# Layer-1 projections with the covariance chain of one batch placed between the products of the next, and the first load for the attention moved into that stage

## What is computed

```
qkv = layernorm(x) @ W_qkv.T + b_qkv          # q, k, v: 16 heads of 8
scores = einsum('bhid,bhjd->bhij', q, k) * D ** -0.5
topk_scores, indices = top_k(scores, int(1024 * 0.3))
masked = full(-inf); masked[indices] = topk_scores
x = x + (softmax(masked) @ v) @ W_out.T + b_out
```

## Time and profile before

| | us |
|---|---|
| median of 3 runs | 3386.67 |
| lowest, highest | 3386.05, 3387.24 |
| the profiled execution, whole time | 3384.95 |
| its span in the trace | 3383.2 |
| layer-1 projections in it | 856 to 1000 |
| layer-1 attention in it | 1000 to about 3040 |

### The profile page before, as it was taken

How to read it: one execution, slowest core, us unless ns; L and a number is a source line. 1 busy time by engine, 2 the same in 40 slices (tenths; PEclk the granted TensorE clock), 3 DMA queues, 4 the chain that set the end, 5 groups by cost and what they waited for, 6 DMA issues and landing times. The chain is left out here.

```text
span 3383.2 us, 74549 instructions
## 1 busy us (share of the span) xinstructions
PE 2601.1 (77%) x23705; PEld 1456.7 (43%) x23705; DVE 2700.5 (80%) x8588; ACT 2383.1 (70%) x3987; POOL 2029.4 (60%) x4543
## 2 busy tenths in 40 slices
PE   3699999669654777777777777775777777758999
PEld 2233333234431444444444444443554454543444
DVE  5788888235438999999999999998999999744444
ACT  2266666533117999999999999997999999822221
POOL 3133333410117999999999999996999989640000
PEclk8699999879665777777778777877777777868999
DMA  5312211000121011001101100110110110010000
GB/s 150 94 47 53 55 49 40 14 25 26 52 63 21 2 18 18 11 9 18 18 2 18 18 12 9 18 18 2 18 18 2 18 18 2 2 33 3 7 7 10
DMA packets 115264, 85.87 MB, mean 25 GB/s; under 512 B 58153, under 2 KB 97339, under 8 KB 114875
## 3 DMA queue, kind: packets, MB, share of 16 engines
q1 hardware_dynamic: 106331, 75.20, 10.4%
q0 software_dynamic: 8192, 4.79, 0.9%
q10 hardware_dynamic: 352, 1.18, 0.1%
HBM read 54.25 MB, written 19.40 MB: 22 GB/s over the span
## 5 line engine op out<-in xcount | busy, mean ns | idle before, releaser
L1285 POOL TENSOR_TENSOR a_near<-a_side,a_z 128x1024 int32<-128x1024 int32 x512 | 968.9, 1892 | 42.6
L1181 PE MATMUL a_ST<-a_qs,a_ks 75*128 75x128 bf16 x4096 | 656.5, 249 | 397.5 <-DVE a_mask L1418 208.6
L1381 DVE MAX8 a_cand<-a_near 128x8 f32<-128x256 f32 x2048 | 810.8, 414 | 0.0
L1181 PEld LDWEIGHTS a_ST<-a_qs,a_ks 75*128 75x128 bf16 x4096 | 459.1, 114 | 564.1 <-DVE a_mask L1418 338.7
L1425 DVE TENSOR_SCALAR_CACHE_REDUCE a_z<-a_S,a_thr 128x1024 f32<-128x1024 f32 x512 | 650.2, 1270 | 33.6 <-POOL a_thr L1261 27.9
L1205 ACT ACTIVATE a_signs<-a_z,a_tiny 128x1024 bf16<-128x1024 f32 x512 | 589.6, 1152 | 73.9 <-DVE a_z L1425 72.4
L1198 ACT ACTIVATE a_signs<-a_S,search 128x1024 bf16<-128x1024 f32 x512 | 572.2, 1118 | 24.3 <-PE a_S L1136 24.2
L1220 ACT ACTIVATE a_eT<-a_ST 128x1024 f32<-128x1024 f32 x512 | 520.2, 1016 | 18.0 <-PE a_ST L1182 17.5
L776 ACT ACTIVATE a_eT<-a_ST 128x512 f32<-128x512 f32 (+3 forms) x768 | 329.2, 489 | 210.0 <-PE a_ST L761 148.6
L1136 PE MATMUL a_S<-a_ks,a_qs 72*128 72x512 bf16 x1024 | 394.4, 475 | 101.4 <-DVE a_z L1425 76.6
L880 DVE TENSOR_REDUCE a_mx<-a_S 128x1 f32<-128x512 f32 (+3 forms) x768 | 381.2, 547 | 77.3 <-PE a_S L748 67.7
(11 more groups left out here) (341 smaller groups left out, 4639.6 us busy)
## 6 DMA issues: line engine op xcount, KB each, us to landing
a_qs<-q_parts SPq DMA_DIRECT2D x174, 64.0 KB
a_ks<-k_parts SPq DMA_DIRECT2D x174, 64.0 KB
a_qs<-a_flip SPq DMA_DIRECT2D x512, 0.8 KB
q_parts<-p_qp SPq DMA_DIRECT2D x48, 128.0 KB, 1.7
k_parts<-p_kp SPq DMA_DIRECT2D x48, 128.0 KB, 1.8
a_qs<-q_parts SPq DMA_DIRECT2D x60, 96.0 KB
a_ks<-k_parts SPq DMA_DIRECT2D x60, 96.0 KB
f_w<-L_ffn_W SPq DMA_DIRECT2D x16, 256.0 KB, 2.8
```

The source lines that it names most:

```text
L1181: pe.matmul(ST[:, block_of], ks[:, base(hl) + kb * P:base(hl) + (kb + 1) * P], qs[:, tile(hl):tile(hl) + P], start=True, stop=False)
L1285: pool.tensor_tensor(near[:, hl % NEARS, :].bitcast(I32), side[:, one].bitcast(I32).broadcast_to([P, SEQ]), z[:, hl % H, :].bitcast(I32), ...
L1381: mm = dve.max(found[:, 8 * g:8 * g + 8], near[:, h2 % NEARS, g * SW:(g + 1) * SW])
```

## The change

`project` is split. `project0` is what it was for layer 0, with the same instructions. `project1` replaces it for layer 1, written out over chunks n = 0 to 7 and over five rounds b = 0 to 4. In round b PE and DVE do the two chunks of batch b, and the covariance chain of batch b - 1 stands in pieces between them; round 0 has no chain, round 4 has only one. To allow that there are four `qf`, two `qcq` and two `mean_bd`; `q_ps` goes from two to one, and the sums, the chain, the applied covariance and the estimates each have a PSUM bank. PE signals the queries and the keys separately (`q_done`, `k_done`). SP stores q ahead of v.

`qs`, `ks` and `v` of the attention are now allocated ahead of `project1`, and SP issues the loads of quad 0 in it, behind the stores of chunk 3, after waiting for the stores of batch 0. In `attention1` the two load calls at the start are gone.

```diff
-            project(nc, k, 1, stats, ln1)
             ctx_all = part.enter_context(nc.sbuf_tensor("ctx1", [P, NT, D], F32))
+            k.qs, k.ks = (part.enter_context(nc.sbuf_tensor(f"a1_{x}", [STACK + SPLIT, 2 * 4 * SEQ], BF16)) for x in ("qs", "ks"))
+            k.v = part.enter_context(nc.sbuf_tensor("a1_v", [P, 2, IB, 4 * (HD + 1)], F32))
+            k.kq_in, k.v_in = (part.enter_context(nc.semaphore(f"a1_{x}_in")) for x in ("kq", "v"))
+            project1(nc, k, stats, ln1)
...
+            normalize(0)
+            for b in range(B + 1):
+                n = CB * b
+                if b > 0:
+                    take_sums(b - 1)
+                if b < B:
+                    normalize(n + 1)
+                if b > 0:
+                    take_means(b - 1)
+                if b < B:
+                    split_q(n)
+                if b > 0:
+                    take_gram(b - 1)
+                if b < B:
+                    add_bias_v(n)
+                if b > 0:
+                    take_cov(b - 1)
+                if b < B - 1:
+                    normalize(n + 2)
+                if b > 0:
+                    weigh(n - 2)
+                if b < B:
+                    split_q(n + 1)
+                if b > 0:
+                    weigh(n - 1)
+                    take_estimates(n - 2)
+                if b < B:
+                    add_bias_v(n + 1)
+                if b > 0:
+                    take_estimates(n - 1)
...
+            def sum_products(n):
+                b, c = n // CB, n % CB
+                if c == 0 and b > 0:
+                    pe.wait_ge(cov_v, COV_V * (b - 1) + 2)
+                for t in range(CT):
+                    mm = pe.matmul(gram_ps, xn[c][:, t, 0:D], xn[c][:, t, :],
+                                   start=(c == 0 and t == 0), stop=(c == CB - 1 and t == CT - 1))
+                mm.then_inc(gram_s, 1)
...
+            for b in range(B + 1):
+                n = CB * b
+                if b < B:
+                    turn(n)
+                    sum_products(n)
+                if b > 0:
+                    weigh_sums(b - 1)
+                if b < B:
+                    queries(n)
+                    keys(n)
+                if b > 0:
+                    weigh_again(b - 1)
+                if b < B:
+                    values(n)
+                if b > 0:
+                    outer(b - 1)
+                if b < B:
+                    turn(n + 1)
+                    sum_products(n + 1)
+                if b > 0:
+                    apply_cov(n - 2)
+                if b < B:
+                    queries(n + 1)
+                    keys(n + 1)
+                if b > 0:
+                    estimate(n - 2)
+                    apply_cov(n - 1)
+                if b < B:
+                    values(n + 1)
+                if b > 0:
+                    estimate(n - 1)
...
+            for n in range(NCH):
+                b, c = n // CB, n % CB
+                cols = slice(c * CW, (c + 1) * CW)
+                sp.wait_ge(qsplit, SPLIT * n + SPLIT)
+                for s in range(SPLIT):
+                    sp.dma_start(k.q_parts[s, b * D:(b + 1) * D, cols], qp[c][:, s, :]).then_inc(stored[c], 16)
...
+                if n == 2 * CB - 1:
+                    for x in range(CB):
+                        sp.wait_ge(stored[x], STORES)
+                    load_quad(sp, k, 0)
+                    load_v(sp, k, 0)
...
-            load(0)
-            load_v(0)
             sp.wait_ge(const, 1)
```

More of the change, by code:

```diff
@@ L391, in _ @@
-            if lead:
-                dve.wait_ge(sd_s, 1)
-                dve.scalar_tensor_tensor(first[:, :], base1[:, :], -Z_KEEP, first[:, :], ALU.mult, ALU.add).then_inc(fin_v, 1)
-                dve.tensor_scalar(step[:, :], base1[:, :], -1.0 / (2 * SEQ * PDF_KEEP), None, ALU.mult).then_inc(fin_v, 1)
-                dve.wait_ge(fin_v, 2)
-                dve.scalar_tensor_tensor(base1[:, :], step[:, :], -SGN_KEEP, first[:, :], ALU.mult, ALU.add).then_inc(fin_v, 1)
-                dve.wait_ge(fin_v, 3)
@@ L406, in _ @@
             act.nop().then_inc(xT_s, 1)
-            if pre is None:
-                act.wait_ge(var_s, NCH)
             act.activation(std[:, :], var[:, :], ACT.Sqrt).then_inc(std_s, 1)
-            scale = QSCALE1 if lead else 1.0
             def project_chunks(b):
@@ L427, in project_chunks @@
-                    act.wait_ge(ksplit, SPLITS * n + SPLITS)
-                    act.activation(kf[c][:, :], k_ps[c % VB][:, :], ACT.Identity, bias=k.bk[layer][:, 0:1])
-                    act.activation(kp[c][:, 0, :], k_ps[c % VB][:, :], ACT.Identity, bias=k.bk[layer][:, 0:1]).then_inc(k_s, 1)
-            if layer == 0:
-                project_chunks(0)
-                project_chunks(1)
-                for c in range(CB):
-                    act.wait_ge(stored[c], free(1))
-                act.wait_ge(blank_s[0], 64)
-                load_pass0(act, k, 0)
-                project_chunks(2)
-                project_chunks(3)
-            else:
-                with act.Fori(0, B) as b:
-                    project_chunks(b)
@@ L446, in _ @@
+                    act.activation(kp[c][:, 0, :], k_ps[c][:, :], ACT.Identity, bias=k.bk[0][:, 0:1]).then_inc(k_s, 1)
+            project_chunks(0)
+            project_chunks(1)
+            for c in range(CB):
+                act.wait_ge(stored[c], free(1))
+            act.wait_ge(blank_s[0], 64)
+            load_pass0(act, k, 0)
+            project_chunks(2)
+            project_chunks(3)
         @block.gpsimd
         def _(pool):
-            for c in range(SPLITS * CB):
+            for c in range(SPLIT * CB):
@@ L452, in _ @@
                     n = b * CB + c
-                    done = SPLITS * CB + SPLITS * n
+                    done = SPLIT * CB + SPLIT * n
                     pool.wait_ge(k_s, CB + n + 1)
@@ L465, in _ @@
                 pe.nop().then_inc(v_done, 1)
-            if lead:
-                for c in range(CB):
-                    pe.nop().then_inc(gram_s, 1)
-                pe.nop().then_inc(est_s, 1)
             with pe.Fori(0, B) as b:
@@ L478, in _ @@
                     mm.then_inc(turned, 1)
-                    if lead:
-                        if c == 0:
-                            pe.wait_ge(est_v, 2 * CB * b + 1)
-                        for t in range(CT):
-                            mm = pe.matmul(gram_ps, xn[c][:, t, 0:D], xn[c][:, t, :],
-                                           start=(c == 0 and t == 0), stop=(c == CB - 1 and t == CT - 1))
-                        mm.then_inc(gram_s, 1)
                     pe.wait_ge(xT_s, n + 2)
@@ L561, in _, with load_quad @@
+            fill(0)
+            store(0)
+            fill(1)
+            store(1)
+            fill(2)
+            store(2)
+            fill(3)
+            store(3)
+            sp.wait_ge(blank_s[1], 64)
+            load_pass0(sp, k, 1)
+            sp.wait_ge(blank_s[2], 64)
+            sp.wait_ge(blank_s[3], 64)
             for c in range(CB):
                 sp.wait_ge(stored[c], free(B))
+def load_quad(sp, k, m):
+    terms = [(x, y, slice((x * SPLIT + y) * HD, (x * SPLIT + y + 1) * HD)) for x in range(SPLIT) for y in range(SPLIT)]
+    at, cols = m // 4 * D + m % 4 * 4 * HD, slice(m % 2 * 4 * SEQ, (m % 2 + 1) * 4 * SEQ)
+    for x, y, rows in terms:
+        sp.dma_start(k.ks[rows, cols].rearrange("d (h t) -> d h t", h=4),
+                     k.k_parts[y, at:at + 4 * HD, :].rearrange("(h d) t -> d h t", d=HD)).then_inc(k.kq_in, 16)
+        sp.dma_start(k.qs[rows, cols].rearrange("d (h t) -> d h t", h=4),
+                     k.q_parts[x, at:at + 4 * HD, :].rearrange("(h d) t -> d h t", d=HD)).then_inc(k.kq_in, 16)
@@ L1105, in _ @@
             sp.wait_ge(kq_in, 16 * DMAS)
-            load(1)
+            load_quad(sp, k, 1)
             sp.wait_ge(v_in, 16)
-            load_v(1)
+            load_v(sp, k, 1)
             for m in range(PAIRS):
```

413 lines of the change are left out of this document (245 added, 168 removed).

## The result

Beside each other on one chip, four executions of each kernel gave 3323.9 us for the changed one (3321.9 to 3324.9) and 3387.0 us for the one before (3386.1 to 3389.4). The ratio is 0.9817, its 95% interval 0.9804 to 0.9829: 63 us gained, where 51.5 were forecast. The time lies at the fast edge of the range, 11 us under the forecast and 0.9 us above the range's lower bound of 3323.

A forecast was written before the change was run, and what follows sets the result against it. No engine was full: a projection batch was bound by hand-overs, products then chain. Rounds 1 to 3 and the last chain gave 31.6 us, with round 0 32.0, with the load 51.5: 3335 us, range 3323 to 3352.

The forecast's parts named there:

- The quad moved: Start of attention1: with quad 0 already loaded, PE starts at DVE's last constant, 19.5 us sooner (bounds 17 to 19.5).
- Round 0: Products of batch 0: the separate signal lets ACT take q one product sooner, 0.4 us gained (bounds 0 to 1).
- Rounds 1 to 3: Layer-1 projections with products and chain interleaved: three rounds of 23.5 us replace three periods of 33.93 us.
- so I expect it to fall about there once a round: PE's clock, at the short matmuls ending each round: it falls and PE starts the next round low, hence 23.5 us.
- the high clock: Rival for rounds 1 to 3: clock stays high, rounds of 22.1, 19.7 and 19.7 us, time 3326 us; chance 0.2.
- SP's 19 issues hidden: SP's queue in the projections: issuing the moved loads takes 6.6 us between chunk 3's and chunk 4's stores, at no cost.
- The rival of the stores behind the quad: Chunk 4's stores wait behind the quad; with the clock high ACT stalls 2.5 us for chunk 6's buffer, 3328; chance 0.05.
- if ACT or DVE waits for stores: A sign in the projections that would show the prediction wrong; no store wait was expected ahead of ACT's chunk 6 copy.
- Round 4: Last covariance chain alone, after the projections: 17.7 us as before, with 1 us less as a bound.
- Attention1 and the rest: Attention1's steps, the experts and layer 0: same instructions, so they count nothing.
- the last rival: Attention1's steps change pace, 0.06 us of play each; 0.12 us a step gives 3396; chance 0.02, 0.01 for a part.
- The loops written out: Projection batch seams: the trace shows the jump costs nothing, so no gain; the skill's rule would give one, size unknown.

The follow-up runs named there:

- e3_before_quad: Kernel before with only the loads of quad 0 moved behind chunk 3's stores, products and chain as before; 3367.0 us, ratio 0.9947.
- e2_quad_late: Changed kernel with the loads of quad 0 issued behind chunk 5's stores in place of chunk 3's; 3320.7 us, ratio 0.9808 to the kernel before.
- e1_quad_back: Changed kernel with the loads of quad 0 put back at the start of attention1; 3335.9 us, ratio 0.9855 to the kernel before.
- e4_est3: Changed kernel with each stretch of 16 short estimate matmuls done three times, same result; 3376.3 us, ratio 0.997 to the kernel before.
- e7: Kernel with the quad behind chunk 5's stores, plus 14 unread 512-column matmuls in PE's waits of the last chain; 3313.7 us, ratio 0.9788.
- e9: Kernel with the quad behind chunk 5's stores, plus filler matmuls and both applied covariances together in the last chain; 3312.2 us, ratio 0.9786.

## Why the prediction was right and wrong

**The quad moved, -19.5.** Right in mechanism and size: -18.9 in the changed kernel and -18.9 alone (e3_before_quad). What is late next is DVE's constants, as said. The first scores come 4.80 us behind the last estimate, where the walk gave 4.2.

**Round 0, -0.4.** -1.6, outside the bounds of 0 to 1. This row holds everything from the start of the span, and in the eleven profiles with the new round 0, which all have the same instructions up to there, its end lies anywhere from 874.3 to 876.7 (877.3 in before, 876.9 in e3_before_quad). So the gain is 0.3 to 3.0 us, and one profile can't tell more.

**Rounds 1 to 3, 23.5 us each.** This is the step that failed, at "so I expect it to fall about there once a round". From e2_quad_late, without the stall, the three rounds are 52.84 us, not 70.5: the term was 17.7 us too large (15.4 in e1_quad_back, with its fall in the second round). The forecast carried the 0.50 of the earlier trace rows over to the new order as if the short matmuls pulled the clock down. In those rows they stand behind a chain of waits, at a clock that had fallen already. In the new order they are 1.8 us long, with products ahead and behind, and the clock passes over them; stretched to 5.4 us they do let it fall (e4_est3). So the observation was right, and the step from it to the new order was not. A fall within the rounds does come in three of the seven profiles, but once in three rounds, in the middle of the second. No run holds the clock low under the new order, so how the halving of a batch divides between overlap and clock is known only from the durations at either level. The walk at the high clock, 22.1 and 19.7, was too slow as well, by 2.6 us at the steady 17.1. The timeline gives part of that: the second pass of the q split, reckoned at the 1.56 us that it took with POOL beside it, starts ahead of POOL's operation here and takes 0.69, which brings the wait ahead of the outer product to 1.58 us, not 2:

```profile
882.42 0.69 DVE L512 TENSOR_TENSOR p_qp<-p_qres,p_qp 128x512 bf16<-128x512 f32 x1
882.43 1.69 POOL L630 TENSOR_TENSOR p_kres<-p_kf,p_kp 128x512 f32<-128x512 f32 x1 [6.56 <-ACT p_kp L621]
883.55 0.48 PE L686 MATMUL p_chain_ps<-p_mean_bdT 16*128 16x128 f32 x2 [1.58 <-DVE p_mean_bdT L542]
...
887.93 0.29 PE L702 MATMUL p_est_ps<-head_of,p_qcq 128*128 128x16 f32 x2
```

and the 16 short matmuls take 1.8 us, not 2.1.

**SP's 19 issues hidden, "no cost, with 2 us to spare".** The 6.6 us were right. The conclusion held for rounds of 23.5 us only. The rival of the stores behind the quad had the right mechanism, the right buffer (chunk 4's, for chunk 6) and the right condition, a high clock. By the prediction's own sign, "if ACT or DVE waits for stores", this part of it was wrong. The rival's price was 2.5 us (its own 47 less 45 gives 2) and it measured 7.0. It had the stores landed 25 us behind the quad's first issue (47 against 22) and ACT wanting the buffer at 23 (45 against 22); in the trace they landed at 23.6 (918.79 against 895.23), and ACT wanted it at 16.7 (911.94, 6.85 us before 918.79). The landing was right, the rounds were not. The stall also let the clock fall, which the rival didn't count. So the two misses are one: shorter rounds bring forward the moment at which the stall begins. A chance of 0.05 for it beside 0.2 for the high clock was not consistent, since by the rival's own condition the one brings the other. That the time lies in the range at all is in part luck: rounds 17.7 us too long in the forecast, and 7.0 us of stall that it had at nothing, stand against each other, and without the stall the time is 3320.7 us (e2_quad_late), below the range.

The rule of the Trainium skill beside it ("DMA: Bandwidth & Descriptors", section on queues, rings and completion order: on each DMA engine a row's descriptors are taken in ring order) agrees with the 14.3 us of the quad's v and with stores that landed behind it. The prediction didn't have the other half, the issues of 1.3 us that became 5.30 and 6.85.

**Round 4, 17.7.** 17.3. The third round ends at 1.00, but the clock falls at 937.4, 1.8 us into the chain, so the bound of 1 us less was not reached. What e7 and e9 gave (3.6 and 6.5 us) was in this term all along.

**Attention1 and the rest, 0.** Right, as far as the runs can tell. Over all other profiles the part behind the first scores takes 2364.4 to 2368.5 us, and 2362.4 in the one of before. The 2.3 us between before and the changed kernel are 0.005 us for each of 512 steps, less than a tenth of the play that the last rival named. They are not tied to the new order, since e3_before_quad has 2.2 of them with the old one, and the four rows ahead of them already give the 63.1 us of the medians. What makes this part 3.5 us longer in e2_quad_late is open: no run here tells apart a different meeting of DVE and POOL from other causes.

**The loops written out.** Whether a written-out stage gains from code that is fetched straight ahead can't be seen by itself in any run here; the account has no row left for it beyond round 0's 1.2 us more than forecast, which is within the play of that row.

## What to carry to other kernels

Place a prefetch behind the last transfer whose buffer somebody will wait for, not merely where the queue is idle: the same 19 loads cost nothing with rounds of 34 us (e3_before_quad) or behind chunk 5 (e2_quad_late), and 7 us with rounds of 17 us behind chunk 3. Walk the schedule once more with the rounds that the change itself makes, since a faster stage moves the deadlines of everything that was reckoned to be hidden. In a serial chain on TensorE the gaps cost twice, as time and as clock; unread full-width matmuls in them gave 3.6 us of 17.3, whereas an order that merely closed the gaps on paper moved the wait to the next hand-over and brought the clock down elsewhere.

## What the runs showed of the hardware that was not expected

- A granted clock of 1.00 fell to 0.50 while PE's records were without a gap, with only 128x16 matmuls in the 5 us before (e4_est3, 892.7). The same matmuls in stretches of 1.8 us between larger ones left it at 1.00 in the changed kernel (889.8 and 893.7 in its first round).
- SP's DMA issues are held back when much is queued: three issues take 1.29 us in a clear queue and 5.30 and 6.85 us behind the quad's 18 small loads, so SP itself is late too.
- Two profiles of one kernel had the clock rise 2 us apart and then fall once in the second round or not at all, worth 2.2 us of 3324. A few us here need several executions, not one profile.
